# A decoder layer on one core: maxima by tensor-scalar with an accumulator, one column for each unit, in place of running maxima and reductions

## The reference

```
# self attention, x: (8, 256, 128), 16 heads of 64
h    = fq_floor(layernorm(x) * fq_round(gamma) + fq_round(beta))
qkv  = fq_floor(h @ fq_round(w_qkv))              # scale from max |h @ w|
dots = fq_floor(q k^T * temp)                     # scale from max |dots|
attn = fq_floor(softmax(dots))
out  = fq_floor(fq_floor(attn v) @ fq_round(w_out))
x    = layernorm(x + out)

# cross attention without softmax, context (8, 512, 128)
x    = layernorm(x + (layernorm(q (k^T v) / sqrt(8) + x) * g + b))

# MLP, 128 -> 512 -> 128
h    = gelu(qlinear(x, W1, b1))
x    = layernorm(x + qlinear(h, W2, b2))

# fq_floor: s = 2^ceil(log2(max|x| / 127)); clip(floor(x / s), -128, 127) * s
# qlinear:  activation scale (max - min) / 255 with a zero point, weights max|w| / 127
```

## Time and profile before

| what | value |
|---|---|
| median of three runs | 481.63 us (481.36 to 481.78) |
| the profiled execution, its own time | 479.8 us |
| its span, first to last instruction | 478.0 us |
| VectorE busy | 420.0 us, 88% |
| ScalarE busy | 350.2 us, 73% |
| TensorE busy (matmuls) | 233.2 us, 49% |
| GpSimd busy | 149.9 us, 31% |
| mean granted TensorE clock | 0.684 of full speed |

### The profile page before, as it was taken

The page is one execution under the profiler, slowest core; times in us unless marked ns, Lnnn a source line. Parts: engine busy times, 40 slices in busy tenths (PEclk is TensorE's granted clock), DMA queues, the critical chain, the costliest instruction groups (busy, mean ns, idle before and its releaser), DMA issues.

```text
span 478.0 us, 6808 instructions
## 1 busy us (share of the span) xinstructions
PE 233.2 (49%) x1541; PEld 106.5 (22%) x1541; DVE 420.0 (88%) x1396; ACT 350.2 (73%) x789; POOL 149.9 (31%) x323
## 2 busy tenths in 40 slices
PE   0269973878677733122222222119997718116031
PEld 0228411323122210011001111003342616102031
DVE  5879897889899999999999999958986985977967
ACT  3678983879899955999999999954776745537133
POOL 2500002001000002888889888870000005520010
PEclk9969995999755555555555555558999775557557
DMA  7500000000344520788888888792001300000002
GB/s 268 145 0 2 0 0 2 22 22 24 132 176 176 191 95 23 163 187 187 187 197 188 182 188 187 165 211 46 2 2 44 106 1 1 0 1 0 0 0 89
DMA packets 84210, 43.16 MB, mean 90 GB/s; under 512 B 69064, under 2 KB 74456, under 8 KB 84059
## 3 DMA queue, kind: packets, MB, share of 16 engines
q1 hardware_dynamic: 82618, 42.69, 34.2%
q10 hardware_dynamic: 1568, 0.21, 0.3%
HBM read 7.75 MB, written 1.58 MB: 20 GB/s over the span
## 4 chain that ended last, share of the span: by engine, by line
DVE 53%; PE 21%; issue 16%; ACT 7%; DMA 1%; DVEq 1%; ACTq 0%
PE ps L475 20%; DVE mem L1308 12%; DVE mem L1055 6%; DVE mem L1213 4%; DVE d_max L1058 4%; DVE mem L1496 2%; DVE row_max L1308 2%; DVE m L1633 2%; DVE m L1634 2%; ACT mem L903 2%; ACT mem L933 1%; DVE r_now L1054 1%; DMA bkv<-in_L_xattn_bv 1%; DVE row_code L1054 1%; DVE neg_max L1054 1%
## 5 line engine op out<-in xcount | busy, mean ns | idle before, releaser
L475 PE MATMUL ps<-mem 64*128 64x256 bf16 (+5 forms) x1188 | 175.0, 355 | 131.7 <-DMA mem<-mem 87.4
L933 ACT ACTIVATE mem<-mem,neg_max 128x256 f32<-128x256 int16 x256 | 126.2, 494 | 13.2 <-DVE neg_max L1054 9.4
L475 PEld LDWEIGHTS ps<-mem 64*128 64x128 bf16 (+3 forms) x1188 | 72.2, 122 | 229.0 <-issue 126.7
L1308 DVE CUSTOM_DVE_ANT_0 mem<-ps,fold,c 128x256 int16<-128x256 f32 x256 | 111.3, 471 | 0.0
L433 POOL TENSOR_SCALAR mem<-mem,r_now 128x256 int16<-128x256 f32 x176 | 80.9, 478 | 80.9 <-DVE r_now L1054 80.8
L1213 DVE TENSOR_TENSOR mem<-mem 128x1024 bf16<-128x1024 bf16 x82 | 54.3, 688 | 6.2 <-ACT mem L873 4.0
L888 ACT ACTIVATE mem<-ps,c 128x1024 bf16<-128x1024 f32 x48 | 48.4, 1294 | 1.6 <-PE ps L475 1.6
L933 ACT ACTIVATION_READ_ACCUMULATOR mem<-mem,neg_max 128x1 f32 x256 | 47.7, 186 | 0.0
L903 ACT ACTIVATE mem<-ps,c 128x1024 int16<-128x1024 f32 x32 | 36.4, 1211 | 13.8 <-DVEq L1250 8.5
L433 POOL TENSOR_SCALAR bv_fine<-mem,r_now 128x256 int16<-128x256 f32 x80 | 36.8, 479 | 5.0 <-DVE r_now L1054 5.0
L1058 DVE TENSOR_REDUCE d_max<-ps 128x1 f32<-128x1024 f32 (+1 forms) x34 | 38.0, 1126 | 0.3 <-PE ps L475 0.3
(11 more groups left out here) (207 smaller groups left out, 380.4 us busy)
## 6 DMA issues: line engine op xcount, KB each, us to landing
mem<-mem SPq DMA_DIRECT2D x64, 256.0 KB, 2.4
mem<-in_L_attn_w_qkv SPq DMA_DIRECT2D x1, 1536.0 KB, 9.3
mem<-in_x SPq DMA_DIRECT2D x2, 512.0 KB, 5.0
mem<-in_x SPq DMA_DIRECT2D x1, 1024.0 KB, 5.5
out<-mem SPq DMA_DIRECT2D x4, 256.0 KB, 2.2
xattn_matrix<-mem SPq DMA_DIRECT2D x1, 512.0 KB
mem<-in_L_attn_w_out SPq DMA_DIRECT2D x1, 512.0 KB, 5.0
mem<-in_L_ffn_W SPq DMA_DIRECT2D x2, 256.0 KB, 4.6
```

The lines of the kernel that those rows point to most:

```text
L475: return te.matmul(o_, l_, r_, start=start, stop=stop)
L933: ins = sc.activation(e_ring[:, u % 4, pos], y_ring[:, u % 4, pos], ACT.Exp, scale=scale_reg, bias=neg_max[:, u % 4, pos:pos + 1], accum_o ...
L1308: ins = ve.tensor_tensor_reduce(y_ring[:, slot, pos], ps[:, 2 * slot + pos // 2, (pos % 2) * N:(pos % 2 + 1) * N], shift, col("g_dots"), - ...
```

## The change

The folds no longer join two tiles. A tensor-scalar multiplies the bf16 tile by 1.0, writes it back in place, and writes the maximum of its columns to one column of `fold_max`, one for each fold (f32, two rows of 64). The tail reduces these 36 or 48 columns. `run_max`, its two memsets, the waits for them, the wait on the fold two before and the two joining folds go. The extremes behind the GELU become two tensor-scalars from the f32 unit, by 1.0 and by -1.0, with the maximum in the accumulator; their elementwise outputs go as bf16 to `hid_c` and to `hid_i`, which are written later anyway.

```diff
-        run_max = at(168, [3, UNIT], BF16)
+        fold_max = at(168, [2, 64], F32)
...
-            pool.wait_ge(sem("gb_codes"), 1)
-            pl.memset(run_max, 0.0).then_inc(sem("run_max_zero"), 1)
-            pool.wait_ge(sem("qkv_scale"), 1)
-            pl.memset(run_max, 0.0).then_inc(sem("run_max_zero"), 1)
...
+            def extreme(col_out, copy, src, op0, fill, op):
+                return ve.tensor_scalar(copy, src, fill, None, op0, op, accum_out=col_out)
...
+                folds = fold_max[:, 1 if phase == "dots" else 0]
...
                         if nth < total - 1:
                             dve.wait_ge(sem(f"{phase}_max_act"), len(acts) + nth + 1)
-                            dve.wait_ge(sem(f"{phase}_folded"), nth + 1)
-                            ve.tensor_tensor(run_max[:, k], run_max[:, k], abs_t[:, k], ALU.max)\
+                            extreme(folds[:, nth:nth + 1], abs_t[:, k], abs_t[:, k], ALU.mult, 1.0, ALU.max)\
                                 .then_inc(sem(f"{phase}_folded"), 1)
 
                 k = (total - 1) % 3
-                others = [j for j in range(3) if j != k]
-                dve.wait_ge(sem(f"{phase}_folded"), total + 2)
-                for j in others:
-                    link(ve.tensor_tensor(run_max[:, k], run_max[:, k], run_max[:, j], ALU.max))
...
-                link(ve.tensor_tensor(run_max[:, k], run_max[:, k], abs_t[:, k], ALU.max))
-                link(ve.tensor_reduce(col("m"), run_max[:, k], AX.X, ALU.max))
+                link(extreme(folds[:, total - 1:total], abs_t[:, k], abs_t[:, k], ALU.mult, 1.0, ALU.max))
+                link(ve.tensor_reduce(col("m"), folds[:, 0:total], AX.X, ALU.max))
...
-            dve.wait_ge(sem("run_max_zero"), 1)
...
-            dve.wait_ge(sem("run_max_zero"), 2)
...
-                ve.tensor_reduce(m8[:, 0, u:u + 1], part, AX.X, ALU.max)
-                ins = ve.tensor_reduce(m8[:, 1, u:u + 1], part, AX.X, ALU.min, negate=True)
+                cols = slice((u % 2) * UNIT, (u % 2 + 1) * UNIT)
+                extreme(m8[:, 0, u:u + 1], hid_c[:, u // 2, cols], part, ALU.mult, 1.0, ALU.max)
+                ins = extreme(m8[:, 1, u:u + 1], hid_i[:, u // 2, cols].bitcast(BF16), part, ALU.mult, -1.0, ALU.max)
```

## The result

The changed kernel takes 513.21 us (median of four runs, 512.92 to 513.91), the kernel before 481.5 (median of four runs, the three of the table above and one more, of 479.68). The ratio is 1.067, with a 95% interval of 1.064 to 1.070. The forecast was 516.5 us in a range of 509 to 528. The profiled execution of after took 512.92 us with a span of 511.1, 33.1 us more than the 478.0 of before.

The account below looks back on a forecast made before the run. VectorE held the chain's largest part, with ScalarE also full in the dots loop. Terms 25.1 + 14.3 - 3.7 + 0.7 - 1.5 = +34.9 us on 479.8 give 514.7, plus 1.8 makes 516.5; range 509 to 528.

Parts of the forecast that it names:

- The price T: Start-to-start time of a 1024-column SBUF tensor-scalar that keeps its maximum: between 1.13 and 1.21 us, taken as 1.17.
- the fast rival: Accumulator keeps the fast mode: bf16 fold 423 ns, extremes' stage -7.8 us, sum -15.1, time 466.5; chance 0.10.
- custom instruction: L1308, reading PSUM with an accumulator: 256 columns every 0.40 to 0.41 us, 0.14 fixed, T's upper end.
- The loops: Folds and maxima on VectorE: dots loop 73.1 against 48.0 us, +25.1; qkv loop 54.5 against 40.2, +14.3.
- The tails: VectorE behind each loop: joining folds -1.41, smaller reduction -1.02, last fold +0.57; -1.86 us a pass, -3.7 for two.
- The memsets: GpSimd: without the first, two VectorE tensor-scalars take 0.48 us, not 1.96, so -1.48; the second 0.
- The extremes: Behind the GELU: 16 x 1.17 = 18.7 us in place of 18.15; +0.7 booked with end effects.
- Profile to median: The earlier median, 481.63, lies 1.8 us above the profiled 479.8; carrying that turns 514.7 into 516.5.
- the form two at a time: Rival: bf16 folds two columns at a time, T about 0.65 us, f32 one at a time: -4.6, 477.0; chance 0.05.
- The slow clock: Rival: slow folds and TensorE at 1.2 GHz in the qkv pass, up to +15.7 us, halfway +8, 524; chance 0.06.

Follow-up runs that it names:

- dots-only run: Kernel before with accumulator folds and the short tail in the dots maximum pass alone; memsets, qkv pass and GELU as before: 503.25 us, 1.046 of before.
- qkv-only run: Kernel before with accumulator folds and the short tail in the qkv maximum pass alone; memsets, dots pass and GELU as before: 492.72 us, 1.023 of before.
- best version: Kernel before with copies for the first three folds instead of memsets, then two running maxima in place of three: 478.68 us, 0.995 of before.

## Why the prediction was right, and where its sizes were off

**The price T.** The direction hung on it, and the step was right: the tensor-scalar that ends in one number for each partition goes at the slow rate of a reduction, 1.14 us for 1024 columns of bf16 or f32, where that rate, 1.04 ns a column, was forecast. The experiments make that the accumulator's doing, 423 against 1212 ns on the same tiles. That the running maximum is carried from column to column was the prediction's reason for it; no run shows the reason, only the rate. The rule of the Trainium skill that spoke against the change ("SBUF — State Buffer", "Who interferes with whom") stands on the same side as the trace: the form with the accumulator shows none of the fast rate. The table of the Trainium skill's "VectorE: DVE Perf Modes", "The perf-mode tier table", which was the fast rival, holds for the plain form, 423 ns here, and not for this one. T was set at 1.17 and measured 1.14. That was the middle between a reduction's 0.06 us of fixed time and the custom instruction's 0.14. The custom instruction was the wrong neighbour: the fixed time is that of a reduction within 0.01, and the read lies wholly beside the next instruction. Over the 98 instructions of the loops and extremes that is 98 x 0.03 = 2.9 us of the sum. It is nearly all by which the sum, 34.9, lies above the 31.7 between the medians. With 1.14 the loops come to 71.7 and 53.5 us, and the profile of after has 71.8 and 53.6.

**The loops.** Both went from their old bound to VectorE, and the qkv loop's slack was used up before the rest was paid, as written. Each loop is borne out alone: +21.9 us (503.25 - 481.37) in the dots-only run, against 23.8 - 1.9, and +11.4 (492.72 - 481.37) in the qkv-only run, against 13.4 - 1.9. With -0.1 for the extremes and -2.2 for the memsets that is 31.0 of the 31.7 between the medians. The missing 0.7 lies within the spread of four medians, and within the 1 us beyond which the two passes would have had to share a cause.

**The tails.** -1.9 each where -1.86 was booked.

**The memsets.** The first was on the chain: -1.48 by the pair's own rows, as forecast, and -2.2 in the run that puts copies in the memsets' place (interval -1.4 to -2.8). The 1.48 is one execution's figure: over the five profiles with a memset the pair is 1.1 to 1.9 us longer than 0.48. The second shows no cost: the code pass beside it takes 49.9 to 50.3 us with it and 49.9 to 50.5 without, the two short executions left out. That this cut was named ahead as the sure gain held up: it is the larger part of the best version's gain.

**The extremes.** +0.2 in place of +0.7, again T.

**Profile to median.** I added 1.8 us to the profiled sum, since the profile of before was faster than its median. That step was right. No term of the sum touches the code pass, which was 1.2 us short in that one execution, so what the terms change is to be added to the median. With T at 1.14 the sum is 34.9 - 2.9 = 32.0, which gives 513.6 from the median, 481.63, and 511.8 from the profiled 479.8; 513.21 was measured. That 514.7, the figure without the 1.8, came out nearer than 516.5 is luck: two errors of opposite sign.

**The rivals.** The fast form and the form two at a time fall with the 1212 ns. The slow clock, which the prediction named as a sign of being wrong by its size, came in part, and the expectation that it would stay up did not hold: the granted clock of the qkv loop is 0.90, 0.89 and 0.86 in the three profiles with the new folds, and was 0.99. All profiles with quick folds keep 1.00 from some 8 us into the loop to its end; with the new folds it falls in the midst, behind TensorE's waits for VectorE. TensorE's busy time there went from 35.2 to 38.9 us in after, far below the 53.6. The dips cost nothing in the profile of after and 1.0 us of VectorE's time in the two others. The prediction's price, +15.7 and half of that, was for a clock down through the whole pass; no run shows that, and it stays untested. By its own rows it is 2 x 35.22 - 54.5 = 15.9.

## What to carry to other kernels

Ask of a replacement by what it is limited, not how many instructions it saves: here an elementwise instruction that also keeps a result for each partition lost the fast rate of the plain one. It cost as much as a reduction, so it gained nothing where it replaced one, and lost 0.5 us each time where it replaced a fold of 0.63. It would pay where one pass takes in two streams, if the accumulator returned what is wanted, which it did not in the form tried. Where two engines are level, as ScalarE and VectorE in the dots loop, making one cheaper gives nothing and making it dearer is paid in full. An engine that is far from the limit can still cost time when it is held back: TensorE's clock fell behind its waits, and in two of three profiles that reached VectorE. Look for gains in the serial tails and at the first diagonal instead. Read a stage's length in several profiled executions before a microsecond of it is explained.

## What the runs showed of the hardware that was not expected

The accumulator read of a tensor-scalar (82 ns) costs no time between two instructions on VectorE: 1.14 us from start to start for 1024 columns, against 1.13 for a reduction. A scalar-tensor-tensor on two f32 streams with an accumulator takes 1.15 us for 1024 columns, no more than one stream. A GpSimd memset that only writes holds up f32 tensor-scalars of VectorE until its end: two that take 0.48 us in the seven profiles without it took 1.5 to 2.4 in five with it.
